# A subtraction after the third maximum, a wait on GpSimd and a norm one round later in a self-attention loop

## The chip, the cores and the metric

The kernel runs on one core of a Trainium2 chip. The time is device microseconds (us) of one execution, as a median over runs. A difference of about 0.3% (7 us here) is what a measurement of this kernel can tell from no change.

## What is computed

Two transformer layers work on x, 8 batches of 512 tokens with 256 channels, all in float32. The change touches only the self-attention of the second layer. Cut to that, the reference is:

```python
HEADS, D_HEAD = 16, 64
def _attn(xq, xc, Wq, Wk, Wv, Wo, bo):
    q = (xq @ Wq).reshape(B, N, HEADS, D_HEAD)      # k, v likewise from xc
    scores = jnp.einsum('bnhd,bshd->bhns', q, k) * D_HEAD ** (-0.5)
    attn = jax.nn.softmax(scores, axis=-1)
    out = jnp.einsum('bhns,bshd->bnhd', attn, v).reshape(B, N, HEADS * D_HEAD)
    return out @ Wo + bo
...
x = _attn(_ln(x, g1, b1), _ln(x, g1, b1), Wq1, Wk1, Wv1, Wo1, bo1) + x
```

Before it stands the first layer (a cross-attention and an MLP), after it a cross-attention and a gated MLP.

## The kernel before

Every float32 product is made of three matmuls on a rounded part and a rest (`mm3`, lines 146 to 148): an operand `hi` is the rounded copy, `lo` is what the subtraction of `hi` from the full value leaves. Making these pairs is the work of ScalarE, VectorE and GpSimd.

**Rounds.** The self-attention loop (`loop3`) runs over 64 pairs of heads, 8 pairs for each of the 8 batches. I call one turn a round, `s`; `p` is its place in the batch, 0 to 7, so round 20 has p 4. Each round works on three pairs at once: on the scores and exponentials of pair `t = s`; on projections, keys, values and row maxima of the next pair `u = s + 1`; and on the product with the values of the pair before, `d = s - 1`. A round has four slots, `j` = 0 to 3, one for each tile of 128 keys. Each engine has its own function with this loop, and executes in the order in which it is written; semaphores are all that ties the engines together.

**The work of a slot.**

- TensorE makes the scores of tile j into banks 0 and 1 in two parts (lines 1290 and 1294). The second part, L1294, needs the negated row maxima of the pair, so the first L1294 of a round waits for `nm3_neg`. Then the product with the values (`values`, six matmuls of `mm3`), and the 128-row scores from which the maxima come (`largest`, L1328). At the end of slot 3 it transposes the maxima (L152). Output projections for two pairs (`output`) stand in slot 3 of odd rounds and slot 1 of even rounds; in slot 1 of an even round VectorE has an addition for them (L1576), in an odd round in slot 3.
- ScalarE takes the exponential of tile j (`exponent`, L1442) into one of two buffers (`pst3`), so exponential j must wait until the rest of tile j - 2 has been taken from that buffer (`p3_lo`). It rounds tiles 1 and 2. In slot 3, after the exponential, it copies four pieces of the output (`OB`, `OA`), then the negated maxima (two copies, which release `nm3_neg`), and, as the next round begins, q (two copies around the next round's first exponential).
- VectorE reads the maxima from PSUM (`largest`, L1528, four in a round) and makes the four rests of the exponentials (`rests`, 128x1024, L162). Before: rest 0 in slot 1, first maximum(s), rest 1 in slot 2 between the second and the third maximum, fourth maximum, rest 2.
- GpSimd rounds tiles 0 and 3, copies the keys (L159, 64x512), and has a chain on the output of an earlier pair in slot 2: multiplication by the reciprocal sums (L1638), rounded copy (L159, 128x512), rest (L165, 128x512).

**The norm of the next batch** is prepared while this one is worked on. Before, in rounds with p 4: its statistics on VectorE in slot 0 (`ln_x_stats`: L239, L243, L246), the power on GpSimd in slot 0 (`ln_pool_rstd`, L256), the scaling on VectorE at the round's end (`ln_scale`, four of L262), the bias addition on GpSimd at its end (`ln_add`, L283). TensorE transposes the result in round p 6.

Of the kernel before, what the change touches and what calls it, by code (L numbers as in the profile page):

```python
# [110 lines left out]
def build(nc, x, ctx_in, par, con, bias, wts, out):  # L111
    es = ExitStack()
    with es:  # L113
# [260 lines left out]
        def ok(v, n):  # L374
            return 0 <= v < n
# [757 lines left out]
        N3 = 8 * NB  # L1133
# [368 lines left out]
        def dve_attention1():  # L1502
            def project(u, n):
                i, src = u % 2, bank(2 + n)
                for h in range(2):
                    hs = src[64 * h:64 * h + 64, :]
                    if n == 0:
                        dve.wait_ge(q3_hi, 2 * u + h)
                        nc.vector.tensor_tensor(qb[i][h][top, :], hs, f32(qa[i][h])[top, :], ALU.subtract  # L1509
                                                ).then_inc(q3_lo.sem, 1)  # L1510
                    else:
                        dve.wait_ge(k3_hi, 2 * u + h)
                        nc.vector.tensor_tensor(ka[i][h][low, :], hs, f32(ka[i][h])[top, :], ALU.subtract
                                                ).then_inc(k3_lo.sem, 1)

            def rests(n):
                if 0 <= n < 4 * N3:
                    if n % 4 in (1, 2):
                        dve.wait_ge(p3_act, 2 * (n // 4) + n % 4 - 1)
                    else:  # L1520
                        dve.wait_ge(p3_pool, 2 * (n // 4) + n % 4 // 3)
                    dve_rest(P3[1][:, n % 4, :], pst3[n % 2], P3[0][:, n % 4, :]).then_inc(p3_lo.sem, 1)

            def largest(u, q, b0):
                dve.wait_ge(b3_mm, 4 * u + q)
                dve.wait_ge(nm3_mm, u - 1)
                dve.wait_ge(m3_set, 0)
                nc.vector.tensor_reduce(M3[:, q, 0:128:64], bank(b0, 2).rearrange("p (a b) -> p a b", a=2),  # L1528
                                        AX.X, ALU.max).then_inc(b3_max.sem, 1)

            def value(u):
                s_ = v3_s[(u // 2) % 2]
                src = bank(v3_bank(u)).rearrange("p (t a e) -> p t a e", t=2, a=2)
                tt = slice(2 * (u % 2), 2 * (u % 2) + 2)
                dve.wait_ge(v3_hi, u)
                for c in range(2):
                    cs = slice(128 * c, 128 * c + 64)
                    m = dve_rest(s_[1][:, tt, :, cs], src[:, :, :, 64 * c:64 * c + 64], s_[0][:, tt, :, cs])
                m.then_inc(v3_lo.sem, 1)

            ahead = dve_attention2()
            for s in loop3:
                t, u, d = s, s + 1, s - 1
                b, p = divmod(max(t, 0), 8)
                more = ok(t, N3)
                if s == 0:
                    after_attention0(dve)
                for j in range(4):
                    if ok(u, N3) and j == 0:
                        project(u, 0)  # L1550
                    if ok(d - 1, N3) and j == 0:
                        k, i = (d - 1) % 2, (d - 1) // 2
                        dve.wait_ge(sum3[k], 2 * i + 1)
                        dve.wait_ge(out3[k], i - 1)
                        nc.vector.reciprocal(SR3[k], SQ3[k]).then_inc(rec3.sem, 1)
                    if j == 0:
                        rests(4 * s - 1)
                    if ok(u, N3) and j == 0:
                        project(u, 1)
                    if ok(u, N3) and u > 0 and j == 1:  # L1560
                        value(u)
                    if ok(u, N3) and j >= 2:
                        largest(u, 2 * j - 3, odd_bank(u))
                    if u == 0 and j == 3:
                        value(u)
                    e = s - 2 if j == 3 else s - 3
                    if j in (1, 2) or j == 3 and not (ok(e, N3) and e % 2 == 1):
                        rests(4 * s + j - 1)
                    if j % 2 == 1 and ok(e, N3) and e % 2 == 1:
                        half = int(j == 1)  # L1570
                        xv = xbuf(2, e // 8)[:, 2 * half:2 * half + 2, :]
                        dve.wait_ge(o3_mm, e - 1 + half)
                        dve.wait_ge(x_bias, 16 + e // 8)
                        if e % 8 > 1:
                            dve.wait_ge(o3_add, e - 3 + half)
                        nc.vector.tensor_tensor(xv, bank(out3_bank(e, half)).rearrange("p (a c) -> p a c", a=2), xv, ALU.add  # L1576
                                                ).then_inc(o3_add.sem, 1)
                        if j == 3:
                            rests(4 * s + 2)
                    if ok(u, N3) and j in (1, 2):  # L1580
                        largest(u, 2 * j - 2, 2)
                    if s == 0:
                        for job in g4[2 * j:2 * j + 2]:
                            dve_weight(job)
                    for _ in range(early4.get(tail3(s, j), 0)):
                        next(ahead)
                    if more and j == 0 and p == 4:
                        ln_x_stats(*after3(b))
                    if s < 0:
                        yield s  # L1590
                if more and p == 4:
                    ln_scale(18 + b, xbuf(*after3(b)), C)
            for _ in ahead:
                pass

        def pool_attention1():
# [22 lines left out]
            for s in loop3:  # L1619
                t, u, d = s, s + 1, s - 1  # L1620
                b, p = divmod(max(t, 0), 8)
                more = ok(t, N3)
# [6 lines left out]
                for j in range(4):  # L1629
# [3 lines left out]
                            pool_copy(kb[u % 2][h][top, :], f32(ka[u % 2][h])[top, :]).then_inc(k3_dup.sem, 1)  # L1633
                    if ok(d - 1, N3) and j == 2:
                        f = d - 1
                        pool.wait_ge(in3[f % 2], 2 * (f // 2) + 1)
                        pool.wait_ge(d3_out, f)
                        nc.gpsimd.tensor_tensor(OA, OA, RS3, ALU.mult).then_inc(mul3.sem, 1)  # L1638
                        pool.wait_ge(mul3, f)
                        pool.wait_ge(o3_mm, 2 * ((f - 2) // 2) + 1)  # L1640
                        pool_copy(o3_s[f % 2][0], OA).then_inc(o3_hi.sem, 1)
                        pool.wait_ge(o3_hi, f)
                        pool_rest(o3_s[f % 2][1], OA, o3_s[f % 2][0]).then_inc(o3_lo.sem, 1)
# [9 lines left out]
                    if j == 2 and more and p == 6:  # L1653
                        pool.wait_ge(v3_mm, 8 * (b - 1) + 7)
                        ln_split_pool(18 + b, ns[(b + 1) % 2])
                    if more and j == 0 and p == 4:
                        ln_pool_rstd(18 + b)
                    if s < 0:
                        yield s
                if more and p == 4:  # L1660
                    ln_add(pool, *after3(b))
            for _ in ahead:
                pass
# [415 lines left out]
```

## Time and profile before

| | us |
|---|---|
| median of 3 runs | 2364.11 |
| lowest, highest | 2357.49, 2364.68 |
| the profiled execution | 2362.01 |
| its span | 2360.2 |

Around the span lie 1.8 us of the profiled execution. In the rows of stretches a round is cut at the start of its first L1294, and the columns are its length, the busy time of each engine with its instructions, the granted clock of TensorE as a share of 2.4 GHz, the share of the DMA engines and GB/s. TensorE is busy 2147.4 us (91% of the span), VectorE 1634.6 (69%), ScalarE 1439.5 (61%), GpSimd 1129.6 (48%). The self-attention loop fills the stretch from about 613 to 1810 us. A row of a timeline gives start, length, engine, line, operation, output and input, count, and in brackets how long the engine was idle before it and what ended that. TensorE's rows overlap, since a matmul's end is modelled; what counts is the distance of the starts.

### The profile page before, as it was taken

To read this page: it belongs to the slowest core of one execution; us is meant where nothing else is said; L and a number is where in the kernel's file an instruction comes from. 1 tells how busy PE (TensorE), PEld (TensorE's weight loads), DVE (VectorE), ACT (ScalarE), POOL (GpSimd) and SP (SyncE) were. 2 spreads that over 40 slices of the span, in tenths; PEclk is the share of its full clock that TensorE was granted. 3 is DMA by queue.
4 is the path that set the end of the run, shared out by engine and by line. 5 is a ranking of instruction groups with operands and counts; after the bars stand their busy time and mean duration, and the time that the engine had idled before them with its cause. 6 is when DMAs were issued, how large, how long until landed. Compare 5 with 4: busy or idle time off the path is not lost. (4 is left out here: it accounts for less than half of the span.)

```text
span 2360.2 us, 31303 instructions
## 1 busy us (share of the span) xinstructions
PE 2147.4 (91%) x11628; PEld 1788.1 (76%) x11628; DVE 1634.6 (69%) x2347; ACT 1439.5 (61%) x2082; POOL 1129.6 (48%) x889
## 2 busy tenths in 40 slices
PE   6867999997799999999999999999998799999998
PEld 4646878786677777777777777777876678899887
DVE  6566667665577777777777777777775776666554
ACT  5435666653477777777777777777775354555431
POOL 2145555545245455454444545445454566666432
PEclk9878999999999999999999999999999899999999
DMA  6710000011000000100000000010012411111000
GB/s 215 278 40 7 21 21 21 10 48 45 27 24 15 24 23 15 36 15 24 23 14 33 14 19 32 15 32 15 14 35 106 169 63 54 54 54 45 10 9 19
DMA packets 84281, 102.67 MB, mean 43 GB/s; under 512 B 29665, under 2 KB 61153, under 8 KB 83617
## 3 DMA queue, kind: packets, MB, share of 16 engines
q1 hardware_dynamic: 84128, 100.66, 12.9%
q8 instruction: 93, 1.52, 0.3%
q14 instruction: 60, 0.48, 0.1%
HBM read 65.50 MB, written 33.82 MB: 42 GB/s over the span
## 5 line engine op out<-in xcount | busy, mean ns | idle before, releaser
L146 PE MATMUL PS<-R 128*128 128x512 f32 (+1 forms) x2944 | 1033.0, 351 | 93.4 <-DVE R L162 59.5
L148 PE MATMUL PS<-R 128*128 128x512 f32 (+1 forms) x2944 | 1003.5, 341 | 0.0
L147 PE MATMUL PS<-R 128*128 128x512 f32 (+1 forms) x2944 | 1002.6, 341 | 0.0
L146 PEld LDWEIGHTS PS<-R 128*128 128x128 f32 x2944 | 569.8, 194 | 208.2 <-DVE R L162 74.2
L156 ACT ACTIVATE R<-PS 64x512 fp32r<-64x512 f32 (+4 forms) x860 | 460.3, 547 | 292.0 <-PE PS L1747 132.6
L148 PEld LDWEIGHTS PS<-R 128*128 128x128 f32 x2944 | 569.2, 193 | 61.9
L147 PEld LDWEIGHTS PS<-R 128*128 128x128 f32 x2944 | 571.3, 194 | 55.3
L162 DVE TENSOR_TENSOR R<-F,R 128x1024 fp32r<-128x1024 f32 (+2 forms) x410 | 481.7, 1179 | 44.5 <-POOL R L159 22.4
L159 POOL TENSOR_SCALAR R<-F 128x1024 fp32r<-128x1024 f32 (+1 forms) x359 | 307.2, 858 | 369.7 <-DVE F L1900 149.4
L1442 ACT ACTIVATE F<-PS 128x1024 f32<-128x1024 f32 x256 | 262.9, 1027 | 184.6 <-DVE R L162 139.2
L159 POOL TENSOR_SCALAR R<-R 64x512 fp32r<-64x512 f32 x128 | 142.8, 1129 | 383.1 <-ACT R L156 383.0
L1528 DVE TENSOR_REDUCE F<-PS 128x2 f32<-128x1024 f32 x256 | 302.1, 1217 | 18.6 <-PE PS L1328 18.4
L162 DVE TENSOR_TENSOR R<-PS,R 128x512 fp32r<-128x512 f32 (+3 forms) x348 | 181.7, 544 | 185.3 <-ACT R L156 184.7
L165 POOL TENSOR_TENSOR R<-F,R 128x512 fp32r<-128x512 f32 (+2 forms) x132 | 241.1, 1830 | 56.1 <-ACT R L156 39.5
L1509 DVE TENSOR_TENSOR R<-PS,R 64x512 fp32r<-64x512 f32 x128 | 88.0, 688 | 238.2 <-ACT R L156 238.2
L156 ACT ACTIVATE R<-F 128x1024 fp32r<-128x1024 f32 (+2 forms) x174 | 157.3, 920 | 66.3 <-PE PS L148 65.9
L156 ACT ACTIVATE F<-PS 64x512 f32<-64x512 f32 (+3 forms) x280 | 160.1, 593 | 49.1 <-PE PS L148 42.2
L1328 PE MATMUL PS<-R 128*128 128x512 f32 x512 | 165.8, 405 | 23.6 <-DVE F L1576 14.9
L1294 PE MATMUL PS<-R 128*128 128x512 f32 x512 | 163.3, 400 | 12.3 <-ACT R L156 11.9
L1290 PE MATMUL PS<-R 128*128 128x512 f32 x512 | 167.8, 409 | 1.9 <-ACT F L1442 1.9
L1638 POOL TENSOR_TENSOR F<-F 128x512 f32<-128x512 f32 x64 | 88.8, 1388 | 108.9 <-DMA F<-sd 108.9
L1328 PEld LDWEIGHTS PS<-R 128*128 128x128 f32 x512 | 88.0, 191 | 61.0 <-issue 31.3
(90 smaller groups left out, 1987.0 us busy)
## 6 DMA issues: line engine op xcount, KB each, us to landing
F<-sd SPq DMA_DIRECT2D x128, 128.0 KB, 2.9
xs<-F SPq DMA_DIRECT2D x16, 512.0 KB, 2.6
F<-xs SPq DMA_DIRECT2D x16, 512.0 KB, 3.6
gd<-F SPq DMA_DIRECT2D x8, 768.0 KB, 3.6
vd<-F SPq DMA_DIRECT2D x8, 768.0 KB, 5.8
R<-gd SPq DMA_DIRECT2D x6, 1024.0 KB, 5.5
R<-vd SPq DMA_DIRECT2D x6, 1024.0 KB, 5.7
F<-in_x SPq DMA_DIRECT2D x8, 512.0 KB, 4.9
```

The lines of the kernel that those rows point to most:

```text
L146: nc.tensor.matmul(o, L[0], Rr[0], start=start, stop=False, skip_group_check=share)
L147: nc.tensor.matmul(o, L[0], Rr[1], start=False, stop=False, skip_group_check=share)
L148: return nc.tensor.matmul(o, L[1], Rr[0], start=False, stop=stop, skip_group_check=share)
L156: return nc.scalar.activation(o, i, ACT.Identity, **k)
L159: return nc.gpsimd.tensor_scalar(o, i, 1.0, 1.0, ALU.mult, ALU.mult)
L162: return nc.vector.tensor_tensor(o, i, f32(hi), ALU.subtract)
L165: return nc.gpsimd.tensor_tensor(o, i, f32(hi), ALU.subtract)
L1290: nc.tensor.matmul(bank(h), ka[i][h][:, kk], qa[i][h], start=True, stop=False)
L1294: m = nc.tensor.matmul(bank(h), kb[i][h][:, kk], qb[i][h], start=False, stop=True)
L1328: m = nc.tensor.matmul(bank(b0 + h), qa[i][h][:, 128 * q:128 * q + 128], ka[i][h], start=True, stop=True)
L1442: nc.scalar.activation(pst3[n % 2], bank(0, 2), ACT.Exp, scale=0.125).then_inc(e3.sem, 1)
L1528: nc.vector.tensor_reduce(M3[:, q, 0:128:64], bank(b0, 2).rearrange("p (a b) -> p a b", a=2), AX.X, ALU.max).then_inc(b3_max.sem, 1)
```

## The change

Three edits, all in the self-attention loop.

1. On VectorE, rest 1 of a round moves from between the second and the third maximum to behind the third. The last round, which has no maxima, keeps its order.
2. On GpSimd, the multiplication at the head of the output chain gets one wait more: on rest 0 of the same round (`p3_lo`).
3. The norm's statistics move from slot 0 of round p 4 to the end of its slot 3; GpSimd's power from slot 0 of p 4 to slot 0 of p 5; the scaling and the bias addition from the end of p 4 to the end of p 5.

```diff
-                    if j in (1, 2) or j == 3 and not (ok(e, N3) and e % 2 == 1):
+                    if j == 1 or j == 2 and not ok(u, N3) or j == 3 and not (ok(e, N3) and e % 2 == 1):
                         rests(4 * s + j - 1)
...
                     if ok(u, N3) and j in (1, 2):
                         largest(u, 2 * j - 2, 2)
+                    if ok(u, N3) and j == 2:
+                        rests(4 * s + 1)
...
-                    if more and j == 0 and p == 4:
+                    if more and j == 3 and p == 4:
                         ln_x_stats(*after3(b))
...
-                if more and p == 4:
+                if more and p == 5:
                     ln_scale(18 + b, xbuf(*after3(b)), C)
...
                         f = d - 1
+                        if more:
+                            pool.wait_ge(p3_lo, 4 * t)
                         pool.wait_ge(in3[f % 2], 2 * (f // 2) + 1)
...
-                    if more and j == 0 and p == 4:
+                    if more and j == 0 and p == 5:
                         ln_pool_rstd(18 + b)
...
-                if more and p == 4:
+                if more and p == 5:
                     ln_add(pool, *after3(b))
```

VectorE from the values' rest of an even round with p 4 (round 4) to the next round's first subtraction on q. L1576 is the addition of the output, L1528 a maximum, L162 with 128x1024 a rest of the exponentials, L239 to L246 the statistics, L262 the scaling. Before:

```order
L1513 TENSOR_TENSOR R<-PS,R 64x512 x2
L239 BN_STATS F<-F 128x6 x4
L243 BN_AGGR F<-F 128x2 x4
L246 TENSOR_SCALAR F<-F 128x4
L162 TENSOR_TENSOR R<-PS,R 128x4x64 x2
L162 TENSOR_TENSOR R<-F,R 128x1024
L1576 TENSOR_TENSOR F<-PS,F 128x512
L1528 TENSOR_REDUCE F<-PS 128x2 x2
L162 TENSOR_TENSOR R<-F,R 128x1024
L1528 TENSOR_REDUCE F<-PS 128x2 x2
L162 TENSOR_TENSOR R<-F,R 128x1024
L262 TENSOR_SCALAR F<-F 128x256 x4
```

The same place after the change:

```order
L1513 TENSOR_TENSOR R<-PS,R 64x512 x2
L162 TENSOR_TENSOR R<-PS,R 128x4x64 x2
L162 TENSOR_TENSOR R<-F,R 128x1024
L1576 TENSOR_TENSOR F<-PS,F 128x512
L1528 TENSOR_REDUCE F<-PS 128x2 x3
L162 TENSOR_TENSOR R<-F,R 128x1024
L1528 TENSOR_REDUCE F<-PS 128x2
L162 TENSOR_TENSOR R<-F,R 128x1024
L239 BN_STATS F<-F 128x6 x4
L243 BN_AGGR F<-F 128x2 x4
L246 TENSOR_SCALAR F<-F 128x4
L1509 TENSOR_TENSOR R<-PS,R 64x512 x2
```

Three maxima now stand in a row ahead of rest 1, one behind it; the statistics stand last, and the scaling has left this round.

GpSimd in the same round with p 4. L256 is the power of the norm, L1638 (L1642 after) the multiplication at the head of the output chain; `p_lo` counts the rests. Before:

```order
L159 TENSOR_SCALAR R<-F 128x1024 [waits d_mm,exp]
L256 TENSOR_TENSOR F<-F 128x4 [waits ln_var]
L1638 TENSOR_TENSOR F<-F 128x512 [waits d_out,rec_in0]
L159 TENSOR_SCALAR R<-F 128x512 [waits o_mm,o_mul]
L165 TENSOR_TENSOR R<-F,R 128x512 [waits o_hi]
```

After:

```order
L159 TENSOR_SCALAR R<-F 128x1024 [waits d_mm,exp]
L1642 TENSOR_TENSOR F<-F 128x512 [waits d_out,rec_in0,p_lo]
L159 TENSOR_SCALAR R<-F 128x512 [waits o_mm,o_mul]
L165 TENSOR_TENSOR R<-F,R 128x512 [waits o_hi]
```

The power has gone to the next round, and the multiplication waits for one semaphore more, here and in the other rounds.

## Rows read from the trace of the kernel before

**Rows 1.** The page's first line.

```profile
span 2360.2 us, 31303 instructions
```

**Rows 2.** Rounds 17, 18, 20, 28, 21, 22: length, busy PE PEld DVE ACT POOL, clock, DMA.

```profile
937.02:954.71 17.69, 17.68 (x90) 14.37 (x90) 13.33 (x16) 13.77 (x20) 8.44 (x7) 1.00 0.06 15
954.71:973.52 18.81, 17.51 (x90) 14.19 (x88) 14.20 (x16) 13.68 (x20) 7.57 (x7) 1.00 0.13 43
991.34:1013.50 22.16, 19.22 (x89) 15.32 (x87) 17.60 (x29) 13.71 (x21) 10.37 (x9) 0.92 0.10 32
1141.95:1162.53 20.58, 17.72 (x90) 14.17 (x88) 17.37 (x29) 13.77 (x21) 9.22 (x8) 1.00 0.12 39
1013.50:1031.08 17.58, 17.53 (x88) 14.40 (x89) 13.33 (x16) 13.74 (x20) 10.40 (x8) 1.00 0.06 16
1031.08:1051.65 20.57, 19.09 (x97) 14.86 (x95) 15.52 (x16) 15.04 (x23) 11.93 (x9) 1.00 0.05 15
```

**Rows 3.** Timeline of VectorE, odd round 17: start, length, line, operation, count, idle.

```profile
946.01 2.35 DVE L1528 TENSOR_REDUCE F<-PS 128x2 f32<-128x1024 f32 x2
948.28 1.22 DVE L162 TENSOR_TENSOR R<-F,R 128x1024 fp32r<-128x1024 f32 x1
...
953.09 1.22 DVE L162 TENSOR_TENSOR R<-F,R 128x1024 fp32r<-128x1024 f32 x1
```

**Rows 4.** Timeline of ScalarE, round 17 and its two borders.

```profile
935.78 2.53 ACT L156 ACTIVATE R<-PS 1x512 fp32r<-1x512 f32 x4
...
949.59 1.03 ACT L1442 ACTIVATE F<-PS 128x1024 f32<-128x1024 f32 x1 [0.90 <-DVE R L162]
950.81 2.27 ACT L156 ACTIVATE F<-PS 1x512 f32<-1x512 f32 x4 [0.20 <-PE PS L148]
953.11 1.19 ACT L156 ACTIVATE R<-PS 1x512 fp32r<-1x512 f32 x2
...
956.12 1.03 ACT L1442 ACTIVATE F<-PS 128x1024 f32<-128x1024 f32 x1
```

**Rows 5.** Timeline of TensorE, round 17: the scores for the third maximum.

```profile
947.37 0.65 PE L1328 MATMUL PS<-R 128*128 128x512 f32 x2
```

**Rows 6.** Timeline of VectorE, even round 18.

```profile
964.40 2.35 DVE L1528 TENSOR_REDUCE F<-PS 128x2 f32<-128x1024 f32 x2
966.67 2.18 DVE L162 TENSOR_TENSOR R<-F,R 128x1024 fp32r<-128x1024 f32 x1
```

**Rows 7.** Timeline of ScalarE, even round 18.

```profile
968.94 1.02 ACT L1442 ACTIVATE F<-PS 128x1024 f32<-128x1024 f32 x1 [1.07 <-DVE R L162]
...
972.28 1.19 ACT L156 ACTIVATE R<-PS 1x512 fp32r<-1x512 f32 x2
```

**Rows 8.** Timeline of TensorE, even round 18.

```profile
966.55 0.62 PE L1328 MATMUL PS<-R 128*128 128x512 f32 x2
...
971.17 0.66 PE L152 MATMUL PS<-F 128*128 128x128 f32 x4 [1.29 <-DVE F L1528]
```

**Rows 9.** Timeline of GpSimd: rest of the output chain in rounds 17 and 18.

```profile
948.45 2.18 POOL L165 TENSOR_TENSOR R<-F,R 128x512 fp32r<-128x512 f32 x1
...
966.46 1.30 POOL L165 TENSOR_TENSOR R<-F,R 128x512 fp32r<-128x512 f32 x1
```

**Rows 10.** Timeline of VectorE in round 20 (p 4): statistics, rest 1, scaling.

```profile
998.40 1.41 DVE L239 BATCH_NORM_STATS2 F<-F 128x6 f32<-128x256 f32 x4
...
1000.47 0.76 DVE L162 TENSOR_TENSOR R<-PS,R 128x256 fp32r<-128x256 f32 x2
...
1005.31 1.32 DVE L162 TENSOR_TENSOR R<-F,R 128x1024 fp32r<-128x1024 f32 x1
...
1010.89 2.10 DVE L262 TENSOR_SCALAR F<-F 128x256 f32<-128x256 f32 x4
```

**Rows 11.** Timeline of TensorE in round 20.

```profile
1003.10 1.03 PE L1328 MATMUL PS<-R 128*128 128x512 f32 x2 [1.84 <-DVE F L1576]
```

**Rows 12.** Timeline of GpSimd in round 20.

```profile
1004.27 1.28 POOL L165 TENSOR_TENSOR R<-F,R 128x512 fp32r<-128x512 f32 x1
```

## The prediction, made before the changed kernel ran

> **What bounds the kernel now.** I read the page first: span 2360.2 us [rows 1], TensorE busy for 91% of it. Then I cut the self-attention loop at the first L1294 of each round [rows 2]. An odd round (17, 937.02 to 954.71) lasts 17.69 us with TensorE busy 17.68: TensorE alone bounds it. An even round (18) lasts 18.81, busy 17.51. A round with p 4 lasts 22.16 at a granted clock of 0.92 (round 20), or 20.58 at full clock (round 28); the same cut gives 22.2 in four batches and 20.6 in the other four. Round 21 (p 5) lasts 17.58, round 22 (p 6) 20.57, since TensorE also transposes the norm there.
>
> Last I followed who releases whom over a round's end. I count from a round's first L1294 and call this moment 0. In the even round the chain is: VectorE's rest 1 starts at 966.67 and takes 2.18 [rows 6]; when it ends, ScalarE may start exponential 3 (968.94, it had waited for VectorE); that and four copies bring ScalarE to the negated maxima at 972.28 [rows 7], and 1.24 later TensorE's L1294 starts the next round (973.52, the end of the stretch in [rows 2]). So from exponential 3 to the negated maxima are 3.34 us, to the next round 4.58, all on one engine, with nothing in between but its own work. In the odd round exponential 3 starts at 949.59, also right behind rest 1 (948.28 plus 1.31 [rows 3, 4]), the copies wait 0.20 for TensorE, the negated maxima start at 953.11 and could release TensorE at 954.35. TensorE comes at 954.71. The slack is 0.36 us, and I take this as the number that decides: **rest 1 opens exponential 3, and exponential 3 leads to the next round.**
>
> **Edit 1, rest 1 behind the third maximum.** It costs VectorE nothing in sum. But rest 1 starts one maximum later; two maxima from start to rest are 2.27 [rows 3], so one is 1.13.
>
> Odd round. The border before round 17 shows how ScalarE begins one: the negations at 935.78 are the first two of four copies that take 2.53 [rows 4], so where ScalarE is what TensorE waits for, exponential 0 stands 2.55 behind the negations and 1.31 behind L1294 (0). VectorE's first maximum is at 8.99 (946.01 less 937.02), the second at 10.12, the third at 11.26. Its scores are made at 947.37 plus 0.65, 11.00: ready [rows 5]. Rest 1 starts at 12.40. Exponential 3 would follow 1.31 later at 13.71, if GpSimd were not reading too. GpSimd's rest starts at 11.43 (948.45) [rows 9] and takes 1.30 when it is first, so it ends at 12.73 and 0.33 us overlap. What an overlap costs VectorE, two rows say: in round 20 GpSimd ends at 1005.55, VectorE's rest had begun at 1005.31 and took 1.32 instead of 1.22, so 0.24 of overlap cost 0.10 [rows 10, 12]; in round 18 1.09 of overlap cost 0.96 [rows 6, 9]. Both are overlap less 0.13, so here 0.20. Exponential 3 starts at 13.91, the negations at 17.25, the next round at 18.49: **0.80 more** than 17.69.
>
> The Trainium skill, "SBUF — State Buffer", section Who interferes with whom, says that a VectorE instruction with two SBUF inputs and a GpSimd instruction that reads SBUF exclude each other for the whole instruction, and that the later one blocks fully. By it the overlap would cost 0.33 here and not 0.20, which over 31 odd rounds is 4 us more than my sum. The two rows agree that the first goes first, and say a little less than the full wait; I go by them.
>
> Even round. Exponential 0 stood at 1.42 (956.12 less 954.70), now at 1.31, so the first maximum comes at 9.59 instead of 9.70 [rows 4, 6], the second at 10.73, and VectorE is ready for the third at 11.86. TensorE made its scores at 966.55, 11.85, in a run that had been held by an addition of VectorE (L1576) which now ends 0.11 earlier: 11.74. With 0.62 for the pair and 0.04 for the release the third maximum starts at 12.40 [rows 8]. Rest 1 starts at 13.53; GpSimd's rest (11.76 to 13.06 by [rows 9]) is over. Exponential 3 starts at 14.84, where it stood at 14.24; the negations at 18.18, the next round at 19.42: **0.61 more** than 18.81. So the edit does take the two readers apart, and saves 0.96; but it gives 1.13 for the maximum and 0.54 for the wait on its scores, less the 0.11. TensorE's wait before the transposes (1.29 [rows 8]) shrinks by about 0.2, and a wait of about 1.2 us before L1294 comes in its place.
>
> A bound from below: if the wait on the scores and the overlap fell away, an odd round would cost 0.60 and an even one 0.07. From above: if in3's landing or the new wait bring GpSimd's rest 0.3 later, the overlap costs up to 0.5 and the odd round 1.1. I take the middle values, since both come from rows of the very rounds.
>
> **Edit 2, GpSimd's wait on rest 0.** Rest 0 starts 1.13 before the first maximum and ends at about 9.08; GpSimd's multiplication starts 2.07 before its rest, at 9.36 in the odd round, released by a DMA. The wait is met before. Zero, in both kinds of rounds; behind it are queued the copy, the rest and the rounding of tile 3, all with over 1 us to spare on their readers. Its bounds are 0 and the 0.3 us used above; it can't gain except in p 4, where the multiplication overlapped rest 0, and that round is counted whole.
>
> **Edit 3, the norm.** In round 20 the statistics held VectorE from 998.40 to 1000.47, ahead of rest 0 and the addition, and TensorE sat 1.84 us for that addition [rows 10, 11]; in that round the clock fell to 1.2 GHz after the wait for 3.4 us, in round 28 not. The scaling (2.10 us at the end) shifted the next negations. Now the statistics (2.07) start when rest 2 ends: at about 15.8 plus 1.2, so 17.0 to 19.1, and VectorE's next work, on q, starts with exponential 0 of the next round at 20.7. Covered, with 1.6 to spare. The scaling (2.1) stands behind rest 2 of round p 5, which starts at 16.07 (953.09) [rows 3] and now ends at 17.3; scaling until 19.4, next work at 19.8. Covered by 0.4. The power (1.0 on GpSimd) fits in its idle time before the multiplication, and the bias addition (2.4) ends 2 us before its next keys. So p 4 becomes a plain even round of 19.42: **2.74 less** in four batches, **1.16 less** in the other four. Round p 5 becomes a plain odd round: 18.49 for 17.58, 0.91 more. If the covers were gone, up to 0.5 of the scaling would show, 4 us in all.
>
> Round p 6 stays at 20.57: ScalarE waits there for TensorE's last values, about 1 us behind exponential 3, so the later rest 1 has room. In p 7 (17.6) the negations and exponential 0 lie 0.12 closer, so it gains that: 0.79 more.
>
> **The sum.** A batch has p 0 and p 2 (2 x 0.61), p 1 and p 3 (2 x 0.80), p 4, p 5 (0.91), p 7 (0.79): 4.52 less 2.74 is 1.8 in four batches, less 1.16 is 3.4 in four. That is 20.6. Round 0 is bound by weights and round 63 has no maxima, less 1.4: **19 us more**. Against the profiled execution's own 2362.0 it is 2381; that execution lies 2.1 below the median, and two of three runs lie above it, one 4.5 below. I say 2380.
>
> **The rivals.**
>
> *The delay of exponential 3 costs nothing, and the norm's gain stands* (faster). For it: ScalarE is only 61% busy over the kernel, and VectorE 69%. Then the plain rounds stay, p 4 becomes 18.81: 3.35 x 4 and 1.77 x 4, 20.5 less, 2341; with the 0.96 of round 18 saved on top in some 30 even rounds, down to about 2312. Against it: ScalarE waited 1.07 and 0.90 us for exactly this rest [rows 4, 7], and 4.58 us of its own work lie between there and L1294. Chance 0.08.
>
> *Half of it* (no difference). The third maximum finds its scores ready and GpSimd does not hold rest 1: plain even rounds cost 0.07, odd 0.60, p 5 0.71, p 7 0.59. The batches come to -0.6 and +0.9, in all about 1 us: 2363. It needs TensorE's scores 0.5 us earlier in its order than in round 18; nothing shows how. Chance 0.12.
>
> *TensorE's clock falls* (slower by more). An even round now has about 1.2 us of waiting at L1294 and 0.6 before the transposes. A single wait of 1.84 at p 4 was followed by 1.2 GHz, at 1.58 us a time (22.16 less 20.58 [rows 2]); the 1.29 of round 18 was not (clock 1.00). If it befalls the 23 plain even rounds of p 0, 2, 4, it is 36 us: 2416; every second one, 2398. It decides when one wait comes near 1.8. Chance 0.08.
>
> *The edit doesn't do what it says*: that is the case for edit 2, which is in the forecast at zero.
>
> **How the numbers follow.** Forecast 0.72, no difference 0.12, faster 0.08, slower by the clock 0.08. The forecast's own range from the bounds is 2368 to 2392. The range takes in the second rival and the lower part of the third, 2360 to 2398, and leaves out the first and the worst of the third. About 0.3%, 7 us, is what a measurement can tell from none. Faster 0.08; within 0.13; slower 0.79.
>
> **What would show it.** Right: round lengths of 18.5 and 19.4 where there were 17.7 and 18.8; TensorE waiting at L1294 for ScalarE in every round but p 6; exponential 3 about 13.9 and 14.8 behind L1294; rest 1 in even rounds 1.22 long; no round of 22 us and no fall of the clock at p 4; four L262 in p 5 done before q's first subtraction. Wrong: even rounds at 18 or below, or ScalarE's wait for rest 1 no longer there. If the rounds are shorter than I say, look at where TensorE makes the scores of the third maximum.

## The result and the profile after

| | before | after |
|---|---|---|
| median | 2363.8 us (4 runs) | 2380.7 us (4 runs) |
| lowest, highest | 2357.5, 2364.7 | 2375.5, 2384.7 |
| ratio, 95% interval | | 1.007 (1.0051 to 1.0089) |
| span of the profiled execution | 2360.2 | 2382.9 |
| self-attention loop, first L1294 of round 0 to that of round 63 | 1186.0 | 1201.1 |

The change makes the kernel 17 us slower; the prediction was 2380, between 2360 and 2398.

Rounds of the changed kernel, cut like [rows 2]: rounds 17, 18, 20, 28, 21, 22 and then the whole loop. The columns are length, busy time of TensorE, its weight loads, VectorE, ScalarE, GpSimd, the granted clock, the DMA share and GB/s.

```profile
949.54:967.83 18.29, 17.48 (x88) 14.31 (x88) 13.51 (x16) 13.75 (x21) 7.50 (x7) 1.00 0.05 15
967.83:987.25 19.42, 17.58 (x89) 14.38 (x89) 13.32 (x16) 13.76 (x21) 8.44 (x7) 1.00 0.13 42
1005.55:1024.97 19.42, 17.59 (x89) 14.38 (x89) 15.20 (x25) 13.75 (x21) 8.40 (x7) 1.00 0.13 41
1157.59:1176.97 19.38, 17.55 (x88) 14.38 (x88) 15.19 (x25) 13.76 (x21) 8.46 (x7) 1.00 0.13 42
1024.97:1043.34 18.37, 17.49 (x89) 14.31 (x89) 14.95 (x20) 13.76 (x21) 8.48 (x8) 1.00 0.05 16
1043.34:1063.78 20.44, 18.97 (x96) 15.01 (x96) 14.99 (x16) 15.20 (x23) 14.22 (x10) 1.00 0.05 15
623.11:1824.25 1201.14, 1108.00 (x5543) 900.56 (x5542) 889.27 (x1120) 877.11 (x1273) 551.32 (x470) 1.00 0.07 22
```

The odd round has gone from 17.69 to 18.29 (18.35 is usual after), the even one from 18.81 to 19.42. The long rounds of p 4, 22.16 and 20.58, are plain ones of 19.4 now, in all eight batches, and the clock no longer falls there. TensorE is busy about 17.5 us of a plain round and waits for ScalarE at its end. Round 22 (p 6) is the exception: 19.0 busy, and there ScalarE's copies wait for TensorE's last values, not for rest 1:

```profile
1060.25 2.27 ACT L156 ACTIVATE F<-PS 1x512 f32<-1x512 f32 x4 [1.04 <-PE PS L148]
```

ScalarE at the end of round 17 and in the even round 18 (start, length, line, operation, count, idle before and what ended it); the rows answer to [rows 4, 7]:

```profile
963.25 1.03 ACT L1442 ACTIVATE F<-PS 128x1024 f32<-128x1024 f32 x1 [2.14 <-DVE R L162]
964.30 2.27 ACT L156 ACTIVATE F<-PS 1x512 f32<-1x512 f32 x4
966.60 2.40 ACT L156 ACTIVATE R<-PS 1x512 fp32r<-1x512 f32 x4
...
982.67 1.02 ACT L1442 ACTIVATE F<-PS 128x1024 f32<-128x1024 f32 x1 [1.78 <-DVE R L162]
```

VectorE in the same rounds; the rows answer to [rows 3, 6]:

```profile
961.81 1.35 DVE L162 TENSOR_TENSOR R<-F,R 128x1024 fp32r<-128x1024 f32 x1
...
980.22 1.23 DVE L1528 TENSOR_REDUCE F<-PS 128x2 f32<-128x1024 f32 x1 [0.56 <-PE PS L1328]
981.36 1.22 DVE L162 TENSOR_TENSOR R<-F,R 128x1024 fp32r<-128x1024 f32 x1
```

TensorE in round 18 and at its end; the rows answer to [rows 8]:

```profile
983.77 0.65 PE L152 MATMUL PS<-F 128*128 128x128 f32 x4 [0.87 <-DVE F L1528]
...
987.25 0.73 PE L1294 MATMUL PS<-R 128*128 128x512 f32 x2 [0.97 <-ACT R L156]
```

Read from the bottom: L1294 waits 0.97 us for ScalarE, whose negations (the first two of the four copies behind the output's) follow without a gap on the output's copies, those on exponential 3, and exponential 3 had waited 1.78 us for rest 1. In the even round it starts 14.84 us behind L1294 (982.67 less 967.83), where the prediction had 14.84; VectorE's third maximum had waited 0.56 for its scores, predicted 0.54; the next L1294 comes at 19.42, predicted 19.42. In the odd round exponential 3 starts at 13.71 (963.25 less 949.54), predicted 13.91.

**A part of the profiles' difference is not the change's.** The spans differ by 22.7 us, the loop by 15.1. Ahead of the loop, in code that both kernels share, the second kernel took 8.0 us more, behind it 0.4 less: the loop's first L1294 comes at 615.06 before and at 623.11 after. Two stretches there show the clock, first of before, then of after:

```profile
320.00:400.00 80.00, 70.72 (x444) 60.93 (x443) 58.09 (x100) 50.67 (x74) 41.73 (x31) 0.98 0.09 30
400.00:480.00 80.00, 74.47 (x495) 66.24 (x494) 53.80 (x85) 52.43 (x73) 43.61 (x31) 1.00 0.02 8
```

```profile
320.00:400.00 80.00, 70.00 (x429) 59.89 (x430) 55.94 (x96) 49.81 (x71) 40.84 (x30) 0.94 0.08 26
400.00:480.00 80.00, 75.14 (x463) 65.94 (x462) 51.41 (x83) 49.82 (x70) 39.94 (x28) 0.93 0.04 12
```

The granted clock was 0.94 and 0.93 there after, 0.98 and 1.00 before; between 320 and 480 us the second kernel falls 6.7 us behind. Single executions of the kernel before, 25 of them in one comparison, lie between 2354.7 and 2370.7. So I compare the length of the loop below, beside the medians.

### The profile page after: what moved, and what is told of

The parts are those of the page before. It is cut to its first block and busy times, and to the rows that moved or that the text cites. A ratio compares the mean times of both kernels' runs of the same rounds, so it can differ in the third digit from the quotient of the medians.

```text
span 2382.9 us, 31303 instructions
## 1 busy us (share of the span) xinstructions
PE 2141.7 (90%) x11628; PEld 1791.6 (75%) x11628; DVE 1617.5 (68%) x2347; ACT 1442.3 (61%) x2082; POOL 1112.7 (47%) x889
## 5 line engine op out<-in xcount | busy, mean ns | idle before, releaser
L148 PE MATMUL PS<-R 128*128 128x512 f32 (+1 forms) x2944 | 1004.5, 341 | 0.0
L148 PEld LDWEIGHTS PS<-R 128*128 128x128 f32 x2944 | 570.3, 194 | 62.6
L159 POOL TENSOR_SCALAR R<-F 128x1024 fp32r<-128x1024 f32 (+1 forms) x359 | 326.5, 912 | 447.7 <-ACT F L1442 154.2
L162 DVE TENSOR_TENSOR R<-F,R 128x1024 fp32r<-128x1024 f32 (+2 forms) x410 | 466.3, 1141 | 44.4 <-POOL R L159 22.8
L1528 DVE TENSOR_REDUCE F<-PS 128x2 f32<-128x1024 f32 x256 | 303.6, 1218 | 33.3 <-PE PS L1328 33.3
L162 DVE TENSOR_TENSOR R<-PS,R 128x512 fp32r<-128x512 f32 (+3 forms) x348 | 181.7, 543 | 193.8 <-ACT R L156 193.4
L165 POOL TENSOR_TENSOR R<-F,R 128x512 fp32r<-128x512 f32 (+2 forms) x132 | 212.3, 1611 | 55.6 <-ACT R L156 40.8
L1294 PE MATMUL PS<-R 128*128 128x512 f32 x512 | 166.7, 407 | 54.4 <-ACT R L156 54.4
L1294 PEld LDWEIGHTS PS<-R 128*128 128x128 f32 x512 | 92.0, 189 | 97.2 <-ACT R L156 81.0
L1642 POOL TENSOR_TENSOR F<-F 128x512 f32<-128x512 f32 x64 | 83.7, 1308 | 116.2 <-DVE R L162 100.3
```

Of the source, the lines that this page charges most:

```text
L148: return nc.tensor.matmul(o, L[1], Rr[0], start=False, stop=stop, skip_group_check=share)
L159: return nc.gpsimd.tensor_scalar(o, i, 1.0, 1.0, ALU.mult, ALU.mult)
L162: return nc.vector.tensor_tensor(o, i, f32(hi), ALU.subtract)
L165: return nc.gpsimd.tensor_tensor(o, i, f32(hi), ALU.subtract)
L1294: m = nc.tensor.matmul(bank(h), kb[i][h][:, kk], qb[i][h], start=False, stop=True)
```

## The experiments

The loop's length is from the first L1294 of round 0 to that of round 63. The medians are of 2 (the runs with rest 1 behind the fourth maximum, and with GpSimd held and one copy less) to 10 executions; every ratio is to the kernel before in the same comparison. The columns odd to p 6 give usual lengths of a round; "even" is p 0 and p 2.

| kernel | median, us | ratio to before, 95% | loop, us | odd | even | p 4 | p 6 |
|---|---|---|---|---|---|---|---|
| before | 2363.8 | | 1186.0 | 17.65 | 18.76 | 22.2 or 20.6 | 20.57 |
| after | 2380.7 | 1.0051 to 1.0089 | 1201.1 | 18.35 | 19.41 | 19.41 | 20.44 |
| rest 1 stays (edits 2, 3) | 2343.1 | 0.9897 to 0.9950 | 1167.4 | 17.7 | 18.76 | 18.8 | 20.56 |
| move alone (edit 1) | 2394.5 | 1.0108 to 1.0154 | 1216.6 | 18.4 | 19.42 | 21.1 | 20.45 |
| wait alone (edit 2) | 2366.9 | 0.9981 to 1.0018 | 1185.7 | 17.7 | 18.76 | 22.2 or 20.6 | 20.57 |
| move in odd rounds (edits 1 in part, 2, 3) | 2367.1 | 0.9999 to 1.0031 | 1187.4 | 18.45 | 18.65 | 18.65 | 20.42 |
| after, one copy less | 2346.1 | 0.9901 to 0.9949 | 1169.0 | 17.75 | 18.81 | 18.81 | 19.9 |
| after, rest 1 behind the fourth | 2481.7 | 1.0440 to 1.0565 | 1302.2 | 19.4 | 20.79 | 20.8 | 24.1 |
| GpSimd held, later norm | 2339.7 | 0.9877 to 0.9926 | 1164.7 | 17.6 | 18.77 | 18.8 | 20.56 |
| GpSimd held, nothing else | 2362.5 | 0.9978 to 1.0016 | 1186.6 | 17.6 | 18.76 | 22.2 or 20.6 | 20.56 |
| held, later norm, one copy less | 2326.5 | 0.9791 to 0.9901 | 1148.0 | 17.6 | 18.16 | 18.16 | 20.0 |
| held, later norm, VectorE negates | 2335.2 | 0.9847 to 0.9908 | 1155.7 | 17.65 | 18.04 | 18.04 | 21.05 |

### Rest 1 stays where it was

```diff
-                    if j == 1 or j == 2 and not ok(u, N3) or j == 3 and not (ok(e, N3) and e % 2 == 1):
+                    if j in (1, 2) or j == 3 and not (ok(e, N3) and e % 2 == 1):
                         rests(4 * s + j - 1)
...
-                    if ok(u, N3) and j == 2:
-                        rests(4 * s + 1)
```

> The changed kernel with edit 1 taken back: rest 1 stands between the second and the third maximum again, the wait of GpSimd and the later norm stay. My theory (rest 1 opens exponential 3, whose 4.6 us of ScalarE work lead to the next round): plain rounds return to 17.7 and 18.8, a round with p 4 is a plain even one of 18.8 instead of 22.2 or 20.6, so 3.4 us less in four batches and 1.8 in four: 20.5 us less than before, about 2343. A rival, that the loss of the whole change comes from the wait of GpSimd or from the later norm: no gain against before, 2364 or more.

Measured: 2343.1 us, 18.6 less in the loop than before, 33.7 less than after. Round 19 (odd), round 20 (p 4), and the loop:

```profile
965.64:983.28 17.64, 17.61 (x89) 14.38 (x90) 13.33 (x16) 13.77 (x20) 8.40 (x7) 1.00 0.07 22
983.28:1002.03 18.75, 17.53 (x89) 14.19 (x88) 15.41 (x20) 13.69 (x20) 7.56 (x7) 1.00 0.11 38
612.20:1779.64 1167.44, 1114.66 (x5543) 897.64 (x5541) 905.79 (x1120) 875.16 (x1273) 558.47 (x470) 1.00 0.08 23
```

With 18.75 the round with p 4 is as long as a plain even one, and the forecast of 2343 is met. The later norm is worth its whole wait and the moved rest loses more than that.

### The move alone

The kernel before with edit 1 of the change.

> The kernel before with edit 1 alone. My theory: plain rounds of 18.35 (odd) and 19.42 (even), 0.7 and 0.6 more; the round with p 4 keeps its wait for the statistics and gets about 0.6 on top. In sum about 4.6 us a batch, 36 us in all, 2399. A rival, that the removed overlap with GpSimd pays for the maximum in even rounds: odd rounds alone lose, 0.7 in 31 of them, 2385 or less.

Measured: 2394.5 us, 30.5 more in the loop, where I expected 36. An odd round, an even one and round 20 (p 4):

```profile
984.58:1002.90 18.32, 17.52 (x89) 14.37 (x89) 13.50 (x16) 13.78 (x21) 7.49 (x7) 1.00 0.07 16
965.15:984.58 19.43, 17.59 (x88) 14.35 (x88) 13.33 (x16) 13.77 (x21) 8.39 (x7) 1.00 0.11 42
1002.90:1024.05 21.15, 17.82 (x88) 14.30 (x89) 17.30 (x29) 13.76 (x21) 10.42 (x9) 1.00 0.11 38
```

The plain rounds are as forecast (18.32, 19.43). The miss is round p 4, in the third row: 21.15 in every batch at full clock, where I had added 0.6 to 22.2 and 20.6. The clock no longer falls there, so the four batches of 22.2 lose 1.06 us each instead of gaining 0.6. The loops of the two parts differ from the kernel before by 11.9 us together (30.5 less 18.6), where both edits in one kernel cost 15.1. They share a gain: each takes the falls of the clock at p 4 away, and together they can do so only once. The p 4 rounds are shorter by 0.25 us on average with the move alone, by 2.58 with the later norm alone and by 1.97 with both, not 2.83. That is 7 us in eight rounds; the odd rounds, 3.6 us shorter in all than the two parts add up to, take half of it back. Why they are is not shown.

### The wait alone

The kernel before with edit 2 of the change.

> The kernel before with edit 2 alone, GpSimd's multiplication behind rest 0. My theory: the wait is met within 0.1 us of the DMA's landing and nothing reads the output chain in a hurry: no difference, 2364, rounds of 17.6 and 18.8. A rival, that the wait makes GpSimd's chain late enough to hold rest 1 in odd rounds too: odd rounds 0.2 us or more longer, 2370.

Measured: ratio 1.000 (0.9981 to 1.0018). The waits of GpSimd, of the changed kernel and of this one (what waited, on what, us in total, times, longest) name the rest 47 times:

```profile
POOL F L1642 <- DVE R L162: 78.2, 47, 2.1
```
```profile
POOL F L1640 <- DVE R L162: 80.9, 47, 2.0
```

So the new wait does end last by the profile, where the prediction had it met before, but nothing comes later by it: in round 17 after the change the rest ends at 958.50 and the multiplication starts at 958.70, 9.16 behind L1294, no later than the 9.36 of before. It costs nothing that this measurement can see, as predicted.

### The move in odd rounds only

```diff
-                    if j == 1 or j == 2 and not ok(u, N3) or j == 3 and not (ok(e, N3) and e % 2 == 1):
+                    if j == 1 or j == 2 and not (ok(u, N3) and s % 2 == 1) or j == 3 and not (ok(e, N3) and e % 2 == 1):
...
-                    if ok(u, N3) and j == 2:
+                    if ok(u, N3) and j == 2 and s % 2 == 1:
                         rests(4 * s + 1)
```

> The changed kernel with rest 1 behind the third maximum in odd rounds only; even rounds keep it before. My theory: odd rounds 18.35, even rounds 18.8 as before, so against the version with rest 1 in its place everywhere (2343) 0.7 us in 31 odd rounds, 22 us: 2365. A rival, that the two kinds of rounds share one slack and a delay in one is paid back in the other: below 2355.

Measured: 2367.1 us, where I expected 2365, and 19.9 more in the loop than with rest 1 in its place. The 31 odd rounds are 0.77 us longer on average, 24 in all. Of that the even rounds pay a little back: 0.12 us each in p 0, p 2 and p 6 and 0.17 in p 4, 4 us in all (18.65 where there were 18.76). The rival, a shared slack, is true in that small part and not below 2355.

### One copy less between exponential 3 and the next round

```diff
-                        act_copy(OA[64:128, :], bank(5)[64:128, :]).then_inc(d3_out.sem, 1)
+                        if d < 2:
+                            m = act_copy(OA[64:128, :], bank(5)[64:128, :])
+                        m.then_inc(d3_out.sem, 1)
```

> The changed kernel with one of the four copies of the output left out from the third pair on (the upper half of the output, OA rows 64 to 127, is not copied, so the output is not the reference's). It takes 0.57 us from ScalarE between exponential 3 and the negated maxima and nothing from another engine's work. My theory: all rounds are as long as ScalarE's chain, so each shrinks by that, 18.35 to 17.8 and 19.4 to 18.85: some 33 us less than the changed kernel, about 2347. A rival, that after the change VectorE or TensorE bounds the rounds: no difference, 2381.

The kernel leaves out the copy of the output's rows 64 to 127. Measured: 2346.1 us, where I expected 2347. Round 17, round 18 and the loop:

```profile
940.04:957.78 17.74, 17.49 (x88) 14.37 (x88) 13.57 (x16) 13.17 (x20) 7.48 (x7) 1.00 0.05 15
957.78:976.61 18.83, 17.59 (x89) 14.38 (x89) 13.33 (x16) 13.17 (x20) 8.42 (x7) 1.00 0.13 43
621.50:1790.47 1168.97, 1108.87 (x5543) 901.14 (x5541) 891.83 (x1119) 842.04 (x1213) 550.90 (x470) 1.00 0.07 22
```

ScalarE lost 0.6 us a round (13.76 to 13.17). Even rounds lost 0.6 with it, odd ones 0.47 on average, p 6 0.53, the loop 32.2. So after the change the round's length goes over these copies, and neither VectorE nor TensorE had anything taken from it. Where that chain begins the run does not tell: in p 6 it begins at TensorE's values, and the round shrinks all the same. That it begins at rest 1 in the other rounds is shown by the runs that move rest 1, the ones above and the next.

### Rest 1 one maximum later still

```diff
-                    if ok(u, N3) and j == 2:
-                        rests(4 * s + 1)
...
+                    if ok(u, N3) and j == 3:
+                        rests(4 * s + 1)
```

The second piece stands right behind the fourth maximum.

> The changed kernel with rest 1 one maximum later still, behind the fourth. The fourth maximum in turn comes 1.13 earlier. Theory: exponential 3 starts 1.13 us later, and the chain from there to the next round has no slack left: odd rounds 18.35 plus 1.13, 19.5, even rounds 19.4 plus 1.13 and in odd rounds perhaps 0.1 less, since GpSimd's rest is over by then; p 6 about 20.9. About 65 us more than the changed kernel, 2445. A rival, that the loss of the change is a fixed cost of breaking the order and not the delay: below 2400.

Measured: 2481.7 us, 37 more than expected. Round 17, round 18, the loop, and ScalarE and VectorE in round 18:

```profile
972.98:992.46 19.48, 17.73 (x89) 14.60 (x88) 13.38 (x16) 13.78 (x21) 8.40 (x7) 0.99 0.06 14
992.46:1013.25 20.79, 18.60 (x88) 14.83 (x88) 13.43 (x16) 13.76 (x21) 7.51 (x7) 0.94 0.12 39
622.53:1924.71 1302.18, 1141.69 (x5543) 923.70 (x5542) 891.37 (x1119) 877.93 (x1273) 544.13 (x470) 0.97 0.07 20
```
```profile
1008.67 1.02 ACT L1442 ACTIVATE F<-PS 128x1024 f32<-128x1024 f32 x1 [3.14 <-DVE R L162]
```
```profile
1004.86 2.59 DVE L1528 TENSOR_REDUCE F<-PS 128x2 f32<-128x1024 f32 x2 [0.57 <-PE PS L1328]
1007.36 2.35 DVE L162 TENSOR_TENSOR R<-F,R 128x1024 fp32r<-128x1024 f32 x2
```

The direction and the odd rounds are right (19.4). In the even round exponential 3 starts 16.21 behind L1294 (1008.67 less 992.46), 1.37 later than after the change, and the round is 1.37 longer: the two maxima in a row take 2.50 from start to rest instead of 2.27, since the fourth waits for its scores, too. The unexpected part is p 6, which was indifferent to the first delay and takes 24.1 now, 3.7 more. VectorE, GpSimd and ScalarE in round 22 (p 6), which starts at 1074.71:

```profile
1091.39 3.91 DVE L162 TENSOR_TENSOR R<-F,R 128x1024 fp32r<-128x1024 f32 x2
```
```profile
1090.72 2.36 POOL L165 TENSOR_TENSOR R<-F,R 128x1024 fp32r<-128x1024 f32 x1
```
```profile
1094.26 1.02 ACT L1442 ACTIVATE F<-PS 128x1024 f32<-128x1024 f32 x1 [4.83 <-DVE R L162]
```

Behind the fourth maximum rest 1 meets GpSimd's rest of the next batch's norm, which runs until 1093.08. The two rests of VectorE take 3.91 from 1091.39, of which the first, rest 1, has 2.78. That is 1.56 more than 1.22 at an overlap of 1.69: the prediction's "overlap less 0.13" once more. Exponential 3 ends at 20.57 (1095.28 less 1074.71) and the copies follow at 20.60, where they started at 16.92 after the change, behind TensorE's values: 3.68 later, the 3.7 of the round. So here the overlap is on the path. The loop is 101 us longer than after the change; 4 x 1.05, 3 x 1.38 and 3.7 are 12.0 a batch and account for 96. Three odd rounds of 21.3 to 21.5 instead of 19.4, one of them (round 19) at a granted clock of 0.90, are most of the rest; over the loop the clock is 0.97.

### GpSimd steps aside instead

Rest 1 stays; in even rounds GpSimd's rest waits for it. With the later norm:

```diff
                         pool.wait_ge(o3_hi, f)
+                        if more and f % 2 == 0:
+                            pool.wait_ge(p3_lo, 4 * t + 1)
                         pool_rest(o3_s[f % 2][1], OA, o3_s[f % 2][0]).then_inc(o3_lo.sem, 1)
```

> The kernel before with the later norm (edit 3), rest 1 where it was, and GpSimd instead of VectorE made to step aside: in even rounds the rest at the end of its output chain waits for rest 1. My theory (the overlap of 1.1 us in even rounds costs 0.96 on the path through exponential 3): rest 1 takes 1.22 in even rounds, the round falls from 18.8 to about 17.9, where TensorE is the bound. With 20.5 for the norm and 0.9 for each of 24 plain even rounds: 42 us less, 2321. A rival, that a later rest of GpSimd holds the copies of the output or the projections: even rounds stay at 18.8, 2343.

Measured: 2339.7 us and even rounds of 18.76, where I expected 2321 and 17.9. **My expectation fell.** ScalarE in the even round 16, then VectorE:

```profile
929.50 1.03 ACT L1442 ACTIVATE F<-PS 128x1024 f32<-128x1024 f32 x1 [0.24 <-PE PS L1294]
931.31 2.27 ACT L156 ACTIVATE F<-PS 1x512 f32<-1x512 f32 x4 [0.78 <-PE PS L148]
933.61 2.40 ACT L156 ACTIVATE R<-PS 1x512 fp32r<-1x512 f32 x4
```
```profile
928.04 1.21 DVE L162 TENSOR_TENSOR R<-F,R 128x1024 fp32r<-128x1024 f32 x1
```

The overlap is gone: rest 1 takes 1.21 (2.01 in round 16 of the kernel before, 2.18 in round 18), and exponential 3 no longer waits for it. But the output's copies now wait 0.78 us for TensorE's last product with the values (L148), which ends at 15.2 us in an even round, since the output projection stands ahead of it. In the kernel before, exponential 3 of round 18 had ended at the same moment: 968.94 and 1.02 are 969.96, the copies started at 969.99. Two chains were equally late there, and I had followed only the one that the trace names.

And round 18 is not the usual round. The same trace has 14 rounds of p 0 and p 2 behind the first batch. In 12 of them exponential 3 ended 0.12 to 0.53 us before the copies started, and the copies waited for TensorE; rest 1 took 1.62 to 2.18 us, the longest in round 18, and the rounds last 18.74 to 18.77 us but for two (18: 18.82, 58: 19.05). ScalarE in round 24, as long as 18.75:

```profile
1083.16 1.03 ACT L1442 ACTIVATE F<-PS 128x1024 f32<-128x1024 f32 x1 [0.76 <-DVE R L162]
1084.45 2.27 ACT L156 ACTIVATE F<-PS 1x512 f32<-1x512 f32 x4 [0.27 <-PE PS L148]
```

In such a round rest 1 does not set the length, and one round read beside round 18 would have shown it.

The same hold in the kernel before, with nothing else, was run to tell the two theories apart:

> The kernel before, only that GpSimd's rest in even rounds waits for VectorE's rest 1. After the run with this wait and the later norm, in which rest 1 fell from 2.18 to 1.21 us and even rounds stayed at 18.77, my theory is a new one: in even rounds the copies of the output start with the end of TensorE's values, at 15.2 us, and the overlap had only filled the wait for that. So no difference here: 2364, even rounds 18.8. The theory of the prediction's text, that the overlap itself is on the path: even rounds 17.9, some 25 us less, 2340.

Measured: 2362.5 us, ratio 0.9997 (0.9978 to 1.0016), even rounds of 18.76. **The overlap of GpSimd and VectorE cost the kernel before nothing**; with the later norm beside it 3 us at most (loop 1164.7 against 1167.4).

### The even rounds without the copies in their way

Two runs take part of ScalarE's work out of the even round, if the chain is values, copies, negations. One copy less (again the copy of rows 64 to 127 is left out):

> The later norm and the hold of GpSimd's rest in even rounds, with one of the four copies of the output left out from the third pair on (output rows 64 to 127 aren't the reference's). New theory, that even rounds run from TensorE's values over ScalarE's copies and negations: even rounds 18.77 less 0.57, 18.2, odd rounds unchanged at 17.6, where TensorE is the bound, p 6 20.0: 18 us less, about 2322. A rival, that even rounds are held by VectorE's maxima: even rounds unchanged, 2340.

Measured: 2326.5 us, even rounds of 18.16, odd 17.6: 0.6 off the even rounds and nothing off the odd ones, where TensorE bounds. And the negations on VectorE, which is idle at the end of an even round:

```diff
-                    if ok(u, N3) and j == 3:
+                    if ok(u, N3) and j == 3 and s % 2:
                         act.wait_ge(nm3_mm, u)
...
+                    if ok(u, N3) and j == 3 and s % 2 == 0:
+                        dve.wait_ge(nm3_mm, u)
+                        dve.wait_ge(c3_mm, 4 * (u - 2) + 3)
+                        dve.wait_ge(k3_clear, u % 2)
+                        for h in range(2):
+                            m = nc.vector.tensor_scalar(qb[u % 2][h][64:65, :], bank(odd_bank(u))[64 * h:64 * h + 1, :],
+                                                        -1.0, None, ALU.mult)
+                        m.then_inc(nm3_neg.sem, 1)
```

> The later norm and the hold of GpSimd's rest, and in even rounds the two negations of the maxima are made by VectorE behind rest 2 instead of by ScalarE behind the copies of the output. If even rounds are set by TensorE's values, then ScalarE's copies (2.28), then its negations (1.24), this takes the copies from between: TensorE is released at about 17.6 and bounds even rounds, too: 17.7 instead of 18.8, p 6 19.5 instead of 20.6. That is 4.3 us a batch, 33 us less than 2340: about 2307. A rival, that the next exponential on ScalarE or VectorE's longer queue takes the place: above 2330.

Measured: 2335.2 us, where I expected 2307 and gave the rival everything above 2330. Even rounds take 18.04, but p 6 takes 21.05. VectorE at the end of round 16 and of round 22 (p 6), and round 22 in whole:

```profile
931.33 1.21 DVE L162 TENSOR_TENSOR R<-F,R 128x1024 fp32r<-128x1024 f32 x1
932.57 1.38 DVE L1587 TENSOR_SCALAR R<-PS 1x512 fp32r<-1x512 f32 x2
```
```profile
1039.88 2.77 DVE L162 TENSOR_TENSOR R<-F,R 128x1024 fp32r<-128x1024 f32 x1
1042.68 1.39 DVE L1587 TENSOR_SCALAR R<-PS 1x512 fp32r<-1x512 f32 x2
```
```profile
1023.08:1044.12 21.04, 19.09 (x97) 14.87 (x95) 17.12 (x21) 14.66 (x22) 14.31 (x10) 1.00 0.05 14
```

In plain even rounds the mechanism holds, 0.7 of the 1.1 us: the negations end at 933.95 and L1294 follows at 934.01, now behind rest 2. In p 6 that rest takes 2.77, beside the norm's split on GpSimd, and the negations stand behind it, so the round is 0.5 longer instead of 1.1 shorter: that is the rival's case, VectorE's longer queue. Its loop is 9 us shorter than that of GpSimd held with the later norm, but the intervals of the two medians overlap (2327 to 2342 and 2335 to 2347). Both are clearly faster than before and after.

## Why the prediction was right

**Rest 1 opens exponential 3 and that leads to the next round.** Shown, for the changed kernel. The rows after have every link in its place. Taking rest 1 alone back gives 33.7 us of the loop, moving it alone costs 30.5, in odd rounds only 0.77 us in each of them, and one maximum more 1.0 and 1.4 a round. For the kernel before it holds in part: in its even rounds TensorE's values come as late as exponential 3 or later, and "with nothing in between but its own work" was wrong, since the copies wait for those values, too.

**Odd rounds, 0.80 more.** Measured 0.70 (18.35 less 17.65), on average 0.72 in the 31. Two terms were 0.2 too high in round 17 (18.29 where 18.49 was forecast). Exponential 0 came 1.19 behind L1294 and not 1.31, since the four copies at the border took 2.40 here, and not the 2.53 of the row that I had used. With it rest 1 began at 12.27 and not at 12.40. And the overlap with GpSimd was 0.27 us and not 0.33 (GpSimd's rest ran from 960.79 to 962.08, by the row below): rest 1 took 1.35, 0.13 more than 1.22, where 0.20 was forecast. The formula itself was good, it gives 0.14 for 0.27.

```profile
960.79 1.29 POOL L165 TENSOR_TENSOR R<-F,R 128x512 fp32r<-128x512 f32 x1
```

By the full exclusion of the Trainium skill ("SBUF — State Buffer", Who interferes with whom) it would have been 0.27. The later one does wait for the first, and 0.13 less than the rows' overlap says.

**Even rounds, 0.61 more.** Measured 0.61 in round 18, and 0.66 against the usual 18.75. But one sentence of the step was wrong: "So the edit does take the two readers apart, and saves 0.96". Taking them apart saves the round nothing, as the held kernels show: rest 1 ends earlier, and the copies still wait for TensorE's values. The 0.96 counts in the time at which exponential 3 starts, 14.84, and no further. The sum came out because the copies at 15.88 are later than the values' 15.2, so that the chain from rest 1 is the whole path then, and because it was made from the chain as it would run between two starts of L1294. Whoever had forecast "GpSimd held" by the same sentence would have been 19 us off in the median, as I was in my expectation.

**Edit 2 at nothing.** Right, ratio 1.000, though the wait is not met before: it ends last 47 times, and costs nothing.

**Edit 3, 2.74 and 1.16 less at p 4.** Measured 2.74 (22.16 to 19.42) and 1.20. The covers (VectorE's idle time into which the norm's work moved) were there. In the changed kernel the statistics start at 1022.48, right behind rest 2, and VectorE then waits 1.67 for its next work, predicted 1.6; the scaling takes 1.37 for four and not 2.10, and leaves 1.26, predicted 0.4:

```profile
1022.48 1.40 DVE L239 BATCH_NORM_STATS2 F<-F 128x6 f32<-128x256 f32 x4
...
1026.16 0.68 DVE L1509 TENSOR_TENSOR R<-PS,R 64x512 fp32r<-64x512 f32 x1 [1.67 <-ACT R L156]
...
1041.91 1.37 DVE L262 TENSOR_SCALAR F<-F 128x256 f32<-128x256 f32 x4
1044.54 0.68 DVE L1509 TENSOR_TENSOR R<-PS,R 64x512 fp32r<-64x512 f32 x1 [1.26 <-ACT R L156]
```

**The sum.** 19 us forecast, 15.1 measured in the loop; the 31 odd rounds, 0.1 less each, are 3, and p 6 at 20.44 instead of 20.57 is 1. Round 0, left out of the sum, became 0.7 shorter, and the plain even rounds cost 1.1 more than forecast in all. That the median came out within 1 us of 2380 is partly luck: the loop is 4 us below the sum, and the medians differ by 17 where the loops differ by 15, well inside the scatter of single executions. Three numbers of the prediction do not agree with each other and carried no weight: the wait before the transposes is "1.29 less about 0.2" in one place and 0.6 in another (measured 0.87), the chances add to 0.80 for slower and are summed up as 0.79, and the lower end of the forecast's own range, 2368, is not worked out, while its bounds from below together give 2363.

**The rivals.** The free delay is refuted by the two runs that isolate the move. Half of it: no, the third maximum did wait 0.56 for its scores in the even rounds and GpSimd did read beside rest 1 in the odd ones. The falling clock did not come at waits of 0.87 and 0.97 in one round (clock 1.00); with rest 1 behind the fourth maximum it did (0.94 in round 18), so it was a fair rival, one more maximum away.

## What to carry to other kernels

When a step moves in one engine's order, cost it from one start of the bounding engine to the next, through every wait on the way; "this overlap goes away, so its length is saved" holds only if no second chain ends at the same moment. A trace names only the later of two releasers, so look for the one that ended just before it, and read the same place in several rounds: in the kernel before, it was the other one in 12 of 14 rounds. And a change of several edits may hide a good one: the later norm alone is worth 18.6 us of the loop, and the moved rest took back more.

## What the runs showed of the hardware

- The same code ahead of the loop ran 8 us longer in one profiled execution than in another, 6.7 of them where the granted clock was 0.94 and 0.93 instead of 0.98 and 1.00.
- At p 4 a single wait of 1.84 us was followed by 1.2 GHz in four of eight batches; the waits there were 1.79 to 1.84 us in all eight, so their length alone does not decide. Two other kernels with the same wait had it in two and in four of eight batches. With the move alone the wait is 1.44 to 1.50, the same rounds last 21.1 and no batch had it. What decides was not tried.
- VectorE's rest of 1024 elements a row (1.22 us alone) lost nearly the whole overlap with a GpSimd rest that had started first: 0.10 for 0.24, 0.13 for 0.27, 0.96 for 1.09 and 1.56 for 1.69 us.
- Four scalings (L262, 128x256) took 2.10 us before and 1.37 after. Single ones (shortest, median and longest in ns, in round 20 before and in round 21 after) tell that one alone was slow:

```profile
L262 DVE TENSOR_SCALAR F<-F x4: 398/403/1140, 1010.9 to 1012.6; 128x256 f32<-128x256 f32 x4
L262 DVE TENSOR_SCALAR F<-F x4: 400/401/403, 1041.9 to 1042.9; 128x256 f32<-128x256 f32 x4
```

Before, GpSimd's rounding of tile 3 had started ahead of them, beside VectorE's rest 2 (1009.75 to 1010.97):

```profile
1010.10 1.78 POOL L159 TENSOR_SCALAR R<-F 128x1024 fp32r<-128x1024 f32 x1 [4.55 <-PE PS L148]
```

The first scaling (from 1010.89) took 1.14 us and ended 0.15 behind the rounding; the three that started behind its end took 0.40 each, as all four do after, where GpSimd is idle. The Trainium skill ("SBUF — State Buffer", Who interferes with whom) says that such an instruction can take a mode in which it excludes GpSimd. That the first scaling waited for the rounding to end agrees with it, but no run isolated it.
